# The second layer's triangle result in bf16: two engines evict from PSUM straight into it

## The reference

```
left  = (left  * lg).astype(bfloat16)            # 256 x 256 x 64
right = (right * rg).astype(bfloat16)
out = einsum('bikh,bjkh->bijh', left, right).astype(float32)   # result of a bf16 einsum
out = layernorm(out, onorm_w, onorm_b) * og      # over the 64 channels h
x = x + einsum('bijh,dh->bijd', out, w_out)
```

## Time and profile before

| | |
|---|---|
| median of 3 runs | 2089.22 us (2088.78 to 2090.52) |
| profiled execution, its own time | 2091.39 us |
| its span in the trace | 2089.3 us |
| PE busy | 1770.6 us (85%) |
| DVE busy | 1319.1 us (63%) |
| ACT busy | 1372.3 us (66%) |
| POOL busy | 1031.0 us (49%) |
| second layer's triangle, from PE's first matmul to the output block's first instruction | 965.37 to 1024.83 us |
| second layer's output block | from 1024.83 us, steady until about 1170 us |

### The profile page before, as it was taken

The page is one execution under the profiler, slowest core; times in us unless marked ns, Lnnn a source line. Parts: engine busy times, 40 slices in busy tenths (PEclk is TensorE's granted clock), DMA queues, the critical chain, the costliest instruction groups (busy, mean ns, idle before and its releaser), DMA issues. The chain is left out here.

```text
span 2089.3 us, 41026 instructions
## 1 busy us (share of the span) xinstructions
PE 1770.6 (85%) x10389; PEld 1045.5 (50%) x10389; DVE 1319.1 (63%) x2920; ACT 1372.3 (66%) x2541; POOL 1031.0 (49%) x1044
## 2 busy tenths in 40 slices
PE   0889997797998899985699799799799998699776
PEld 0444454685554444444355477643344444588533
DVE  7566666124763677775977388466377778344675
ACT  0577876365996777774599566477478787244554
POOL 0267678003991677786899200089122223000599
PEclk9999998898999999998899899999899999899999
DMA  7357876774996265647499666189557776845599
GB/s 327 124 184 236 245 232 216 271 297 169 365 367 235 97 189 168 193 135 264 146 357 366 231 226 207 35 321 385 175 157 227 237 236 216 296 174 228 193 398 373
DMA packets 326947, 496.15 MB, mean 237 GB/s; under 512 B 22828, under 2 KB 188463, under 8 KB 320439
## 3 DMA queue, kind: packets, MB, share of 16 engines
q1 hardware_dynamic: 326838, 494.93, 68.4%
HBM read 285.12 MB, written 197.13 MB: 231 GB/s over the span
## 5 line engine op out<-in xcount | busy, mean ns | idle before, releaser
L809 POOL TENSOR_TENSOR lo<-xn,hi 128x512 f16<-128x512 f32 x192 | 224.1, 1167 | 373.5 <-DVE hi L736 231.9
L601 PE MATMUL ps<-w_heads,hi 64*128 64x256 f16 x3072 | 292.8, 273 | 11.7 <-POOL lo L809 4.7
L1118 ACT ACTIVATE O<-ps 128x512 f32 (+1 forms) x144 | 151.7, 1054 | 189.3 <-PE ps L1042 189.3
L750 DVE SCALAR_TENSOR_TENSOR sig<-ps,largest,sig 128x512 f32<-128x512 f32 x256 | 180.7, 746 | 145.4 <-ACT sig L664 144.5
L664 ACT ACTIVATE sig<-ps,largest 128x512 f32<-128x512 f32 x384 | 246.1, 692 | 32.2 <-PE ps L601 23.3
L1355 POOL TENSOR_TENSOR shared<-O,out_rs 128x128 f32<-128x128 f32 (+1 forms) x112 | 76.3, 683 | 371.0 <-DVE out_rs L1255 370.0
L645 ACT ACTIVATE zs<-ps,shift 128x512 f32<-128x512 f32 x192 | 132.0, 687 | 192.9 <-PE ps L569 188.9
L601 PEld LDWEIGHTS ps<-w_heads,hi 64*128 64x128 f16 x3072 | 153.2, 95 | 169.3 <-DVE sig L750 67.0
L1403 PEld LDWEIGHTS ps<-ident,shared 128*128 128x128 f32 (+1 forms) x1024 | 120.2, 133 | 224.8 <-issue 96.8
L1403 PE MATMUL ps<-ident,shared 128*128 128x128 f32 (+1 forms) x1024 | 160.8, 282 | 76.6 <-POOL shared L1355 49.2
L601 PE MATMUL ps<-w_heads,lo 64*128 64x256 f16 x1536 | 212.8, 272 | 0.0
(11 more groups left out here) (168 smaller groups left out, 3787.6 us busy)
## 6 DMA issues: line engine op xcount, KB each, us to landing
shared<-left_right SPq DMA_DIRECT2D x34, 2048.0 KB, 12.0
shared<-gate SPq DMA_DIRECT2D x224, 256.0 KB, 4.6
gate<-gates SPq DMA_DIRECT2D x96, 512.0 KB, 2.9
x_dram<-shared SPq DMA_DIRECT2D x192, 256.0 KB, 4.3
shared<-x_dram SPq DMA_DIRECT2D x192, 256.0 KB, 4.7
xs<-x_dram SPq DMA_DIRECT2D x64, 512.0 KB, 4.2
left_right<-stage SPq DMA_DIRECT2D x64, 448.0 KB, 5.9
left_right<-shared SPq DMA_DIRECT2D x64, 448.0 KB, 5.9
```

Of the source, the lines that this page charges most:

```text
L601: last = pe.matmul(PAIR[row][:, g, kb * S:kb * S + S], tokens[half, q % 8, at:at + P], k["w_heads"][half, part, :], start=(step == 0), sto ...
L750: dve.scalar_tensor_tensor(dst, pair(row, 1), k["largest"][:, 1:2], factor, ALU.mult, ALU.mult).then_inc(pair_read.sem, 1)
L809: pool.tensor_tensor(lo[:, q % 8, :], xn[:, q % 2, :], hi[:, q % 8, :], ALU.subtract).then_inc(c["lo_done"].sem, 1)
L1118: act.activation(o_of(ch), ps[h % 4 // 2][:, h % 2, :].rearrange("p (b g i) -> p b g i", b=2, g=2), ACT.Copy).then_inc(c["o_copied"].sem, 1)
```

## The change

For the layer with `low` = BF16, `O` is allocated as bf16 in place of float32, with the same shape. The tile `rounded` and POOL's part of the triangle block are gone. ACT evicts the even channels from PSUM into `O`, DVE the odd ones, each in one instruction per channel. PE waits for the engine that read the bank: `o_copied` for even channels, `o_stored` for odd ones. In the output block the code is the same, and `bn_stats` and `center` now read a bf16 `O`. The other layers keep their instructions.

```
-            O = ctx.enter_context(nc.sbuf_tensor(f"O{n}", [P, 2, HALF, 2, H], F32))
+            O = ctx.enter_context(nc.sbuf_tensor(f"O{n}", [P, 2, HALF, 2, H], low))
...
-        rounded = ctx.enter_context(nc.sbuf_tensor(f"rounded{n}", [P, 4, 2 * S], BF16)) if rounded_first else None
...
-        def rounded_of(slot):
-            return rounded[:, slot].rearrange("p (b g i) -> p b g i", b=2, g=2)
+        def result(h):
+            return ps[h % 4 // 2][:, h % 2, :].rearrange("p (b g i) -> p b g i", b=2, g=2)
...
-                pe.wait_ge(c["o_copied"].sem, c["o_copied"](ch - 3))
+                if rounded_first:
+                    copied = c["o_stored"] if h % 2 else c["o_copied"]
+                    pe.wait_ge(copied.sem, copied(t * HG + (s * HG + h) // 2 - 1))
+                else:
+                    pe.wait_ge(c["o_copied"].sem, c["o_copied"](ch - 3))
...
-            def spread_out(ch):
-                dve.wait_ge(c["o_copied"].sem, c["o_copied"](ch + 1))
-                dve.tensor_copy(o_of(ch), rounded_of(ch % 4)).then_inc(c["o_stored"].sem, 1)
+            def round_odd(t, s, h):
+                ch = channel(t, s, h)
+                dve.wait_ge(c["tri_done"].sem, c["tri_done"](ch + 1))
+                dve.tensor_copy(o_of(ch), result(h)).then_inc(c["o_stored"].sem, 1)
 
             if rounded_first:
-                for ch in range(1, H, 2):
-                    spread_out(ch)
+                with dve.Fori(0, turns) as t:
+                    for s in range(2):
+                        for h in range(1, HG, 2):
+                            round_odd(t, s, h)
...
-        if rounded_first:
-            @block.gpsimd
-            def _(pool):
-                with pool.Fori(0, turns) as t:
-                    for s in range(2):
-                        for h in range(0, HG, 2):
-                            ch = channel(t, s, h)
-                            pool.wait_ge(c["o_copied"].sem, c["o_copied"](ch + 1))
-                            pool.tensor_copy(o_of(ch), rounded_of(h % 4)).then_inc(c["o_moved"].sem, 1)
...
-                    for h in range(HG):
+                    for h in range(0, HG, 2 if rounded_first else 1):
                         ch = channel(t, s, h)
                         act.wait_ge(c["tri_done"].sem, c["tri_done"](ch + 1))
-                        if rounded_first:
-                            spread = c["o_stored"] if h % 2 else c["o_moved"]
-                            act.wait_ge(spread.sem, spread(t * HG + (s * HG + h) // 2 - 1))
-                            act.activation(rounded[:, h % 4], ps[h % 4 // 2][:, h % 2, :], ACT.Copy).then_inc(c["o_copied"].sem, 1)
-                        else:
-                            act.activation(o_of(ch), ps[h % 4 // 2][:, h % 2, :].rearrange("p (b g i) -> p b g i", b=2, g=2),
-                                           ACT.Copy).then_inc(c["o_copied"].sem, 1)
+                        act.activation(o_of(ch), result(h), ACT.Copy).then_inc(c["o_copied"].sem, 1)
```

## The result

The changed kernel takes 2109.4 us (median of 4 runs, 2105.19 to 2113.92), the kernel before 2089.0 us in the same comparison: a ratio of 1.010 with a 95% interval of 1.0076 to 1.0124. It is slower by 20 us, 1.0%. The forecast was 2082.8 us, 6 us faster, in a range of 2080 to 2090. It was wrong in its sign. The profiled execution took 2113.92 us, its span is 2112.1 us.

What follows compares the result with a forecast made beforehand. The second pass bounds the second layer's triangle block, the last load close behind. Gain 6.7 us there less 0.3 us in the output block is 6.4, so 2089.22 to 2082.8 us, range 2080 to 2090.

Steps and rivals of the forecast that it cites:

- the price of what is added: Triangle block, second layer: 32 spread bf16 evictions each on ACT (1042 ns) and DVE (1027 ns), together 0.545 us a channel.
- the 2-byte spread write is dearer: Rival, triangle evictions: 2-byte spread writes cost 1.3 us on both engines, 3.2 us of gain lost, 2086.0 us; chance 0.10.
- The bound before: Second layer's triangle block: second pass bounds at 0.79 us a channel, with the fourth group's load coming out even.
- The sum by groups: Triangle block as four groups of 16 channels: output block starts at 1018.1 in place of 1024.8, gain 6.7 us.
- group 4: Last 16 channels of the triangle block: start at 1008.1 after PE idles 4 us for their load, end at 1017.8.
- The clock: PE before group 4: 4 us of idling do not cost the full clock; if they do, 1.9 us.
- Two writers collide: Rival, triangle block: ACT and DVE writing `O` hold each other up, 1.59 us a pair, no change, 2089; chance 0.14.
- The output block: Block after the triangle: `center` at 1055 to 1159 ns stays hidden, statistics keep their price, 0.3 us lost at the start.
- POOL as the new bound: Rival, output block: mixed-operand `center` above 1197 ns makes POOL the bound, put at 1400 ns, 2095.8 us; chance 0.10.
- faster statistics: Rival, output block's start: DVE's statistics speed up with 2-byte input, 2.1 us more gain, 2080.7 us; chance 0.06.

Runs made afterwards that it cites:

- paired runs: Changed kernel, each engine evicting two neighbouring channels at once, half the tokens per instruction, `O` in bf16: 2083.25 us; with four PSUM places per pair 2080.04 us.
- float32 run: Changed kernel with `O` in float32 and the rounding to bf16 left out: 2084.38 us, ratio 0.998.
- run with four places for a pair: Changed kernel with paired-channel eviction, four places in PSUM for a pair in place of two: 2080.04 us, ratio 0.9963.
- run with the third buffer: Paired-channel eviction with four PSUM places, plus a third buffer for group loads so they are issued earlier: 2078.41 us, ratio 0.9937.

## Why the prediction was wrong

The step that failed is the price of what is added. The prediction took the float32 form of ACT's spread eviction (1042 ns) and 692 + 335 ns on DVE as the price of the bf16 form, and gave 0.10 to "the 2-byte spread write is dearer", priced at 1.3 us. The mechanism of that rival was the right one; its price is 2.30 us on one engine alone and 2.4 to 2.5 with both. No row before showed a 2-byte element written apart from its neighbour: all spread writes there were float32, or (POOL's into the stage) had runs. The text argued from the line alone, that a bf16 output at 256 bytes pays as a float32 one does, and took the float32 row both as its value and as its upper bound, with only DVE's slowest cast above. The bound had no room for an effect of the element's size, and even the rival that named the effect had 1.3 us for it, which would have given 2086.0.

- *The bound before* (second pass, with the last load close behind): right. The paired runs show the load as the next bound, as forecast.
- *The sum by groups*: its order was right for 4-byte elements (PE waits for group 4: 3.2 us in the float32 run, forecast 4), and group 4 started 42.6 us after PE's first matmul, forecast 42.7. From there to the end of the block it took 12.6 us, forecast 10.0: 2.5 us too low, because of the clock and the collision below. With 2.4 us per eviction it lost its meaning: the loads are hidden.
- *The clock*: wrong. After the wait of 3.2 us in the float32 run the granted clock was 0.50; the earlier trace rows had shown a longer idle with the clock still up, and I took that as a rule. The length of the idle alone does not decide it: in the run with four places for a pair PE had been idle since 999.75 and the clock was still 1.00 in 1003 to 1004. What decides it stays open.
- *Two writers collide*: the prediction had 1.59 us a pair and 2089 us for it. It is real, but smaller: in the float32 run PE makes the third group, eight pairs, in 9.03 us, 1.13 us a pair. An eviction goes from 1042 to 1310 ns in float32, and in bf16 the starts go from 2.30 to 2.4 or 2.5 us apart. The row that was held against it, ACT's 1023 to 1122 ns in the other layers, did not test it: DVE's copies there write another tile, densely. The Trainium skill, "SBUF — State Buffer", in the section that was named there, has ACT wait for no other engine; ACT's 1310 ns beside DVE's spread writes, against 1042 without them, are at odds with that, and the measurement decides. What the two share is the tile they write and the PSUM they read. How they collide was not taken apart further.
- *The output block* (`center` under 1197 ns, statistics at their old price, 0.3 us): right. POOL as the new bound did not happen, nor faster statistics. PE's last matmuls start 151.1 us after the block's start (1046.42 to 1197.53) against 150.8 before.

## What to carry to other kernels

Before a tile that is written in a scattered order is narrowed to 2 bytes, look at how many neighbours one instruction writes: a single bf16 in its own 16-byte line cost 2.3 us per 512 values where a float32 cost 1.0 and a pair of bf16 in one 4-byte word 0.6. If the layout must have the scattered index innermost, let one instruction carry two neighbours of that index (here two channels from two PSUM banks); the strided PSUM read was free. And where a price is taken from a row of another element size, the size is one of the unknowns, and the range must say so.

## What the runs showed of the hardware that was not expected

- A visit to a 16-byte line of SBUF that leaves a 4-byte word incomplete costs 4.41 ns on ACT and on DVE alike, worked out from steps of 4 and 8 elements; with whole words 1.75 ns on ACT, where that is not hidden by the engine's own pace (597 ns for 512 values).
- A bf16 run of two at an odd place costs 1308 ns, at an even place 598 ns.
- Two engines that evict from PSUM with scattered writes into one tile slow each other: 1042 to 1310 ns in float32 on ACT.
- In the float32 run PE stood idle for 3.2 us and began again at 1005.09 with a granted clock of 0.50 (1.2 GHz), which rose between 1010 and 1011. In the run with the third buffer it stood idle for 2.55 us and began again at 1.00 (2.4 GHz). In the run with four places for a pair it stood idle for 5.50 us, with 1.00 still granted in 1003 to 1004, more than 3 us into the idle, and began again at 0.50.
